# Routing steps of VectorE placed ahead of the weighted sums, and the fetch, columns and weight loads of the overflow blocks reordered, in a fused attention and mixture-of-experts kernel

## The reference

```
x = x + xattn(layernorm(x), ctx)          # x: 4 x 512 x 512, ctx: 4 x 512 x 256
x = x + ffn(layernorm(x))

xattn:  q = ln_head(x @ Wq + bq), 16 heads of 32
        k, v from ctx[:, :-16]  (Wk, Wv); k2, v2 from ctx[:, -16:]  (Wkv_dca)
        out = (softmax(q k^T / sqrt(32)) v + softmax(q k2^T / sqrt(32)) v2) @ Wo + bo
ffn:    E, TOP_K, F, FS = 64, 6, 352, 704;  N = 2048 tokens, C = 2 * N * TOP_K / E = 384
        scores = softmax(x @ gate_w.T); the 6 best of 64, renormalised
        token t goes to slot pos of its expert (counted in token order), dropped if pos >= C
        expert: (silu(rows @ w_gate.T) * (rows @ w_up.T)) @ w_down.T, times the weight,
        added to the token's row
        plus a shared expert of width 704 over all tokens
```

## Time and profile before

| | |
|---|---|
| runs | 1756.02, 1766.42, 1767.89 us; median 1766.42 us |
| the profiled execution | 1762.85 us, of which the span of instructions is 1761.1 us |
| busy in the span | PE 1693.0 us (96%), PEld 1539.8 (87%), DVE 1090.3 (62%), ACT 1028.3 (58%), POOL 757.9 (43%) |
| mean granted clock of TensorE | 0.982 of full speed |
| 830 to 1660 us (experts) | PE busy 830.00 of 830.00 us |
| 1660 to 1761 us (last items and thirds) | PE busy 78.19 of 101.00 us |

### The profile page before, as it was taken

One profiled execution on the slowest core, in us unless ns is written; L12 is line 12 of the kernel. 1 busy time (PEld: TensorE's weight loads), 2 busy tenths in 40 slices (PEclk: granted clock), 3 DMA queues, 4 the chain that ended last, 5 costly groups with the idle time before them and its releaser, 6 DMA issues. The chain is left out here.

```text
span 1761.1 us, 35834 instructions
## 1 busy us (share of the span) xinstructions
PE 1693.0 (96%) x11782; PEld 1539.8 (87%) x11782; DVE 1090.3 (62%) x2157; ACT 1028.3 (58%) x1871; POOL 757.9 (43%) x719
## 2 busy tenths in 40 slices
PE   4899999999999999999999999999999999999995
PEld 3588888888888888989999999999999999999984
DVE  7555656777566665443666666666666666666664
ACT  4567766666545553222566666666666666666664
POOL 7513222334223230242245555555555555455554
PEclk8899999999899999999999999999999999999997
DMA  5543433433222532312577777777777777777766
GB/s 189 160 117 91 119 105 97 121 95 98 83 84 79 177 107 87 122 38 86 181 227 232 209 214 226 218 210 223 223 216 205 228 221 213 222 232 206 215 198 212
DMA packets 149083, 289.87 MB, mean 165 GB/s; under 512 B 29199, under 2 KB 66319, under 8 KB 139649
## 3 DMA queue, kind: packets, MB, share of 16 engines
q1 hardware_dynamic: 116112, 238.21, 41.9%
q0 software_dynamic: 32880, 50.51, 13.7%
HBM read 243.73 MB, written 64.52 MB: 175 GB/s over the span
## 5 line engine op out<-in xcount | busy, mean ns | idle before, releaser
L2188 POOL DMA_INDIRECT out<-y,ids_s x128 | 209.9, 1640 | 280.3 <-ACT y L2323 254.8
L2448 PE MATMUL ps<-xt_hi,gu_hi 128*128 128x256 f32 (+1 forms) x1856 | 303.5, 285 | 0.6 <-issue 0.6
L2448 PE MATMUL ps<-xt_lo,gu_hi 128*128 128x256 f32 (+1 forms) x1856 | 289.8, 278 | 0.0
L2448 PE MATMUL ps<-xt_hi,gu_lo 128*128 128x256 f32 (+1 forms) x1856 | 289.2, 278 | 0.0
L2223 DVE TENSOR_TENSOR gu_lo<-raw_gu,gu_hi 128x1408 fp32r<-128x1408 f32 (+2 forms) x132 | 214.6, 1625 | 112.5 <-ACT gu_hi L2220 109.3
L1121 ACT ACTIVATE prob<-ps 128x512 f32<-128x512 f32 x256 | 152.2, 597 | 191.4 <-PE ps L1428 169.6
L2448 PEld LDWEIGHTS ps<-xt_hi,gu_hi 128*128 128x128 f32 (+1 forms) x1856 | 250.6, 181 | 9.0 <-issue 3.0
L2448 PEld LDWEIGHTS ps<-xt_lo,gu_hi 128*128 128x128 f32 (+1 forms) x1856 | 244.4, 181 | 0.0
L2448 PEld LDWEIGHTS ps<-xt_hi,gu_lo 128*128 128x128 f32 (+1 forms) x1856 | 244.2, 181 | 0.0
L2168 POOL DMA_INDIRECT xg<-h_rows,ids_g x128 | 191.6, 1497 | 115.2 <-POOL ids_g L2163 50.6
L2280 ACT ACTIVATE h_hi<-h 128x256 fp32r<-128x256 f32 (+1 forms) x240 | 100.6, 419 | 224.0 <-DVE h L2349 223.4
(11 more groups left out here) (316 smaller groups left out, 3000.3 us busy)
## 6 DMA issues: line engine op xcount, KB each, us to landing
raw_gu<-in_w_gu SPq DMA_DIRECT2D x71, 1408.0 KB, 6.7
raw_d<-in_w_d SPq DMA_DIRECT2D x71, 512.0 KB
raw_d<-in_w_d SPq DMA_DIRECT2D x71, 192.0 KB
qs<-qk_rows SPq DMA_DIRECT2D x192, 64.0 KB, 2.2
ks<-qk_rows SPq DMA_DIRECT2D x192, 64.0 KB, 2.0
xa<-in_x SPq DMA_DIRECT2D x16, 256.0 KB, 3.0
qk_rows<-k_hi SPq DMA_DIRECT2D x16, 256.0 KB, 2.2
qk_rows<-k_lo SPq DMA_DIRECT2D x16, 256.0 KB, 2.5
```

What stands on the lines that cost most here:

```text
L2188: pool.indirect_dma_start(out=out, out_offset=bass.IndirectOffsetOnAxis(B.ids_s[:, p, k:k + 1], 0), in_=B.y[:, p, k, :], in_offset=None, b ...
L2448: last = pe.matmul(gu_banks(it, c)[half], gu_columns(w, it, half, d, c), x[:, x_p, d, 0:W], start=i == 0, stop=i == len(steps) - 1)
```

## The change

Heads, DVE: in the second quarter of a unit `route_mask` moves ahead of `weighted(n)`; in the third `route_code` ahead of `weighted(n + 1)`; in the fourth `maxima(n + 4, 1)` ahead of `route_slots`. Heads, PE: in unit 10, the only one with a turn of K and no Q product, the turn of K of tile 15 is made after `third_key` instead of before it. After unit 15 the last head's four `weigh` steps come before the first output product and its two waits. Experts: in `scatter` the copy of the row numbers is made before the wait for the scatter before. Thirds: POOL gathers one block further ahead (`gather(3)` right behind item 63's scatters, `gather(b + 4)` in the body), and copies a block's columns behind the scatter of the block before; ACT makes the high part of T0's down weights before item 63's results instead of after them; SP loads the gate and up part of `b + 3` first and then the down part of `b + 2`, each with its own read of the expert number.

```diff
@@ heads, DVE
                 maxima(n + 2, 1)
                 route_top(u - 6)
+                route_mask(u - 6)
                 weighted(n)
-                route_mask(u - 6)
 
                 maxima(n + 3, 0)
                 scales(u)
                 maxima(n + 3, 1)
                 take_pos(u - 6)
+                route_code(u - 6)
                 weighted(n + 1)
-                route_code(u - 6)
 
                 maxima(n + 4, 0)
                 rest(u + 5, k_full, k_hi, k_lo, k_high, k_low, k_out)
+                maxima(n + 4, 1)
                 route_slots(u - 6)
-                maxima(n + 4, 1)
                 route_weights(u - 6)
                 weighted(n + 2)
@@ heads, PE
                 half1(n + 2)
                 route_pos(u - 6)
-                k_turned(u + 5)
+                if tile(u + 6):
+                    k_turned(u + 5)
                 third_key(n + 2)
+                if not tile(u + 6):
+                    k_turned(u + 5)
                 fourth_key(n + 2)
...
             item = net.item
+            weigh(HEADS - 1, 0)
+            weigh(HEADS - 1, 1)
+            weigh(HEADS - 1, 2)
+            weigh(HEADS - 1, 3)
             pe.wait_ge(at_lo.sem, at_lo.value(WAIT1, 1))
             pe.wait_ge(h2T_in.sem, h2T_in.value(WAIT1 - 1, 1))
             wo_half(WAIT1, 0)
-            weigh(HEADS - 1, 0)
-            weigh(HEADS - 1, 1)
             wo_half(WAIT1, 1)
-            weigh(HEADS - 1, 2)
-            weigh(HEADS - 1, 3)
@@ items, POOL: scatter, after
         p = it.half
+        pool.tensor_copy(B.ids_s[:, p, 0:nb], slots_of(it, B.ids)).then_inc(s_copied.sem, 1)
         ...
             pool.wait_ge(added.sem, added.value(it.expert - 1, 16 * nb))
-        pool.tensor_copy(B.ids_s[:, p, 0:nb], slots_of(it, B.ids)).then_inc(s_copied.sem, 1)
...
             thirds["gather_first"](pool, 2)
+            thirds["columns"](pool, FIRST)
             scatter(pool, it)
+            thirds["gather_first"](pool, 3)
             thirds["y_freed"](pool)
@@ items, ACT: after
             thirds["act_x"](act, FIRST + 1)
+            thirds["act_d"](act, FIRST)
             results(it)
-            thirds["act_d"](act, FIRST)
@@ thirds, SP
-        def load(e, b, gu_done, d_done):
-            ...
+        def load_gu(b, done, turn):
+            e = expert(sp, b)
+            sp.wait_ge(done.sem, done.value(turn, 2))
+            sp.dma_start(B.raw_gu[...], ins["w_gu"][...]).then_inc(gu_in[b.p].sem, 16)
+
+        def load_d(b, done, turn):
+            e = expert(sp, b)
+            sp.wait_ge(done.sem, done.value(turn, 1))
+            sp.dma_start(B.raw_d[...], ...)       # two of them
         for k in range(2):
-            load(expert(sp, FIRST + k), FIRST + k, ...)
-        load(expert(sp, FIRST + 2), FIRST + 2, (gu_lo.sem, gu_lo.value(0, 2)), (d_lo.sem, d_lo.value(0, 1)))
+            load_gu(FIRST + k, S.gu_lo, LAST_ITEM.weights - 1 + k)
+            load_d(FIRST + k, S.d_lo, LAST_ITEM.weights - 1 + k)
+        load_gu(FIRST + 2, gu_lo, 0)
 
         def body(b):
-            e = expert(sp, b + 3)
-            load(e, b + 3, (gu_lo.sem, gu_lo.value(b.j + 1, 2)), (d_lo.sem, d_lo.value(b.j + 1, 1)))
+            load_gu(b + 3, gu_lo, b.j + 1)
+            load_d(b + 2, d_lo, b.j)
@@ thirds, POOL
+    def columns(pool, b):
+        e = expert(pool, b)
+        pool.tensor_copy(B.wsl3[:, b.p:b.p + 1], B.w[...]).then_inc(w_copied.sem, 1)
+        pool.tensor_copy(B.ids3s[:, b.p:b.p + 1], B.ids[...]).then_inc(s_copied.sem, 1)
...
-            pool.wait_ge(xt_ready.sem, xt_ready.value(0, 1))
+            pool.wait_ge(xt_ready.sem, xt_ready.value(k - 2, 1))
...
         def body(b):
-            e = expert(pool, b)
-            pool.tensor_copy(B.wsl3[...]) ; pool.tensor_copy(B.ids3s[...])
-            pool.wait_ge(xt_ready.sem, xt_ready.value(b.j + 1, 1))
-            gather(pool, b + 3)
+            pool.wait_ge(xt_ready.sem, xt_ready.value(b.j + 2, 1))
+            gather(pool, b + 4)
             ...        # wait for the scatter of b - 1, y_free, wait for y: as before
                 compute_op=ALU.add).then_inc(added.sem, 16)
+            columns(pool, b + 1)
```

More of the change, by code:

```diff
@@ L2608, in sync @@
     def sync(sp):
-        def load(e, b, gu_done, d_done):
-            src = ins["w_d"][bass.ds(e, 1)].rearrange("a f n -> (a f) n")
-            sp.wait_ge(*gu_done)
+        def load_gu(b, done, turn):
+            e = expert(sp, b)
+            sp.wait_ge(done.sem, done.value(turn, 2))
             sp.dma_start(B.raw_gu[:, b.p].rearrange("p a n -> p (a n)"),
                          ins["w_gu"][bass.ds(e, 1)].rearrange("a p n -> p (a n)")).then_inc(gu_in[b.p].sem, 16)
-            sp.wait_ge(*d_done)
+        def load_d(b, done, turn):
+            e = expert(sp, b)
+            src = ins["w_d"][bass.ds(e, 1)].rearrange("a f n -> (a f) n")
+            sp.wait_ge(done.sem, done.value(turn, 1))
             sp.dma_start(B.raw_d[:, b.p, 0:2, :], src[0:2 * P, :].rearrange("(c p) n -> p c n", p=P)).then_inc(d_in[b.p].sem, 16)
@@ L2619, in sync @@
         for k in range(2):
-            load(expert(sp, FIRST + k), FIRST + k, (S.gu_lo.sem, S.gu_lo.value(LAST_ITEM.weights - 1 + k, 2)),
-                 (S.d_lo.sem, S.d_lo.value(LAST_ITEM.weights - 1 + k, 1)))
-        load(expert(sp, FIRST + 2), FIRST + 2, (gu_lo.sem, gu_lo.value(0, 2)), (d_lo.sem, d_lo.value(0, 1)))
+            load_gu(FIRST + k, S.gu_lo, LAST_ITEM.weights - 1 + k)
+            load_d(FIRST + k, S.d_lo, LAST_ITEM.weights - 1 + k)
+        load_gu(FIRST + 2, gu_lo, 0)
         def body(b):
-            e = expert(sp, b + 3)
-            load(e, b + 3, (gu_lo.sem, gu_lo.value(b.j + 1, 2)), (d_lo.sem, d_lo.value(b.j + 1, 1)))
+            load_gu(b + 3, gu_lo, b.j + 1)
+            load_d(b + 2, d_lo, b.j)
         each(sp, body)
@@ L2637, in gather @@
             bounds_check=N - 1, oob_is_err=False).then_inc(rows_in[b.p].sem, 16)
+    def columns(pool, b):
+        e = expert(pool, b)
+        pool.tensor_copy(B.wsl3[:, b.p:b.p + 1], B.w[:, bass.ds(e * CB + 2, 1)]).then_inc(w_copied.sem, 1)
+        pool.tensor_copy(B.ids3s[:, b.p:b.p + 1], B.ids[:, bass.ds(e * CB + 2, 1)]).then_inc(s_copied.sem, 1)
     def gather_first(pool, k):
@@ L2653, in body @@
         def body(b):
-            e = expert(pool, b)
-            pool.tensor_copy(B.wsl3[:, b.p:b.p + 1], B.w[:, bass.ds(e * CB + 2, 1)]).then_inc(w_copied.sem, 1)
-            pool.tensor_copy(B.ids3s[:, b.p:b.p + 1], B.ids[:, bass.ds(e * CB + 2, 1)]).then_inc(s_copied.sem, 1)
-            pool.wait_ge(xt_ready.sem, xt_ready.value(b.j + 1, 1))
-            gather(pool, b + 3)
+            pool.wait_ge(xt_ready.sem, xt_ready.value(b.j + 2, 1))
+            gather(pool, b + 4)
             if b.q:
@@ L2673, in body @@
                 compute_op=ALU.add).then_inc(added.sem, 16)
+            columns(pool, b + 1)
         many = each(pool, body)
         for p in range(2):
-            pool.wait_ge(rows_in[p].sem, (many + (4 - p)) // 2 * 16)
+            pool.wait_ge(rows_in[p].sem, (many + (5 - p)) // 2 * 16)
         pool.wait_ge(S.added.sem, S.added.value(LAST_ITEM.expert, 16 * nb))
@@ L2720, in scalar @@
         for p in range(2):
-            loads = (many + (4 - p)) // 2
-            act.wait_ge(gu_in[p].sem, loads * 16)
-            act.wait_ge(d_in[p].sem, loads * 32)
+            act.wait_ge(gu_in[p].sem, (many + (4 - p)) // 2 * 16)
+            act.wait_ge(d_in[p].sem, (many + (3 - p)) // 2 * 32)
         act.sem_inc(act_passed, 1)
@@ L2804, in tensor @@
         each(pe, body, many)
-    return dict(how_many=how_many, sync=sync, gather_first=gather_first, y_freed=y_freed, gpsimd=gpsimd, act_gu=act_gu, act_d=act_d,
+    return dict(how_many=how_many, sync=sync, gather_first=gather_first, columns=columns, y_freed=y_freed, gpsimd=gpsimd, act_gu=act_gu, act_d=act_d,
                 act_x=act_x, silu=silu, high=high, scalar=scalar, dve_gu=dve_gu, dve_x=dve_x, dve_d=dve_d, mix=mix,
```

## The result

The changed kernel takes **1803.74 us** (median of 4 runs, 1797.64 to 1807.54), the kernel before 1765.72 in the same comparison: ratio **1.023**, 95% interval 1.0199 to 1.0261. It is slower by 38 us where 8 us less were forecast. The profiled execution's span is 1803.2 us instead of 1761.1, and the mean granted clock 0.957 instead of 0.982.

What follows compares the result with a forecast made beforehand. PE was taken to bound heads and expert items, POOL and its indirect DMAs the last 50 us. Terms -2.6 - 6.3 + 6.9 - 1.2 - 2 = -5.2 us from 1762.85 gave 1758 us, range 1747 to 1773.

Steps and rivals of the forecast that it cites:

- The routing ahead of the weighted sums: Heads, units 11 to 15: route_mask and route_code ahead of the sums make PE wait, +6.9 us (0 to +15).
- argument for a clock that stays up: Heads, against a fall in unit 10: the units after it have the same order and the clock is up.
- Rival 3: Units 11 to 15: new waits lower the clock, 5.5 us a fall; two give 1769 us, five 1785; chance 0.15.
- The turn of K: Unit 10: PE's 0.85 us wait for scaled K goes and the clock stays up, -6.3 us together.
- the strict reading: Unit 10: clock falls only when PE has been idle, so the wait isn't the cause; 1763.5 us, chance 0.22.
- The maxima ahead of the slots: Heads, units 6 to 9: PE's four waits for DVE's last maxima go, -2.6 us.
- Behind unit 15: After the heads: earlier weigh steps fill PE's h2T wait; second output product starts sooner, -1.2 us (0 to -2.5).
- Thirds: POOL's chain at the end: earlier scatters and T3 gather, T1's scatter starts sooner, -2 us (0 to -4).
- The other terms: Maxima -2.6, turn of K -6.3, behind unit 15 -1.2 and thirds -2 us: all the forecast gains.

Runs made afterwards that it cites:

- the filled kernel: Changed kernel plus seven and four unread score products on PE before the second and third quarter's weighted sums, units 10 to 15: 1765.43 us, ratio 0.9984.
- the single fall: Kernel before with route_mask ahead of weighted(n) in unit 12 only: 1773.95 us, ratio 1.0055.
- the thirds alone: Kernel before with only the edits behind the heads (scatter's copy; the thirds' fetches, columns and weight loads): 1759.72 us, ratio 0.9962.
- the kernel with both moves: Kernel before with only route_mask ahead of weighted(n) and route_code ahead of weighted(n + 1): 1808.57 us, ratio 1.0229.
- the code alone: Kernel before with only route_code ahead of weighted(n + 1): 1781.75 us, ratio 1.0111.
- the mask alone: Kernel before with only route_mask ahead of weighted(n): 1811.04 us, ratio 1.0279.
- the kernel with the small filling: Changed kernel plus 3 and 2 unread score products before the second and third quarter's weighted sums, from unit 10 on: 1773.13 us, ratio 1.0028.
- the old turn of K: Kernel before with only the maxima ahead of the slots and the edits behind the heads: 1764.24 us, ratio 1.0001.

## Why the prediction was wrong

**The routing ahead of the weighted sums (+6.9 us) is the step that failed**, and it failed by what it left out. As waits it was right: the filled kernel against the one without both moves shows 1.7, 1.3, 1.3, 1.3 and 1.6 us for units 11 to 15, 7.2 us together. Missing were unit 10 (+1.5 us, which I had passed over) and 1.3 us in units 6 to 9. PE's wait for pv came to 8.3 us where some 8 were forecast, but that is luck: I had two new waits a unit, and in units 12 to 15 there is one, longer than the mask. But the term was taken as the whole price, with nothing in it for the clock, which made some 42 us more (changed against filled, from unit 10 to the items) and was left to a rival with a chance of 0.15. Its rows were on the table: the earlier trace rows show a fall behind a wait of 0.85 us, and I had just worked out two new waits of 1 us or more for each of five units, in the same thin stretch (in the event PE met one a unit: by the third quarter its own work was slow, and DVE was ahead of it). The prediction's argument for a clock that stays up was that it is up in the units after 10, in the same order. But PE's waits for the sums there are 0.49, 0.22, 0.23 and 0.22 us; the new ones, 1.86 and 1.58 to 1.59, are over three times as long.

**Rival 3 happened, and its price was mis-sized too.** Five falls were to give 1785 us; five came, and it was 1804. I took 5.5 us a fall from unit 10, where it begins in the third quarter and lasts 13.7 us. A fall that begins at the second quarter's sums lasts until the next unit's output product, 23.9 us, and costs 10.2 us (unit 13, changed against filled). Price and length are in line, at about 0.4 us lost per us of low clock: 0.43 there, 0.40 for the single fall (8.2 of 20.5 us), 0.38 in unit 10 of the kernel before (6.1 less the wait of 0.85, of 13.7 us). From unit 15 on the changed kernel has 37.1 us of low clock, 3.0 of them of the fall before, against 6.8 in the filled one, and loses 11.8: 0.39. The new fall in unit 10 is cheaper, 2.3 us for 10.2 us, and why stays open. I should have asked where the fall starts and what ends it, instead of carrying over one sum.

**The turn of K (-6.3 us) was right as a sum, in the unit.** 38.5 to 32.4 us in unit 10 is -6.1, of which the wait is 0.85; at its old place the clock falls again. The Trainium skill (TensorE: Matmul & The Clock Gate, "What's actually happening") ties the low clock to an idle TensorE; by the strict reading that I weighed, a wait of 0.85 us with work on both sides would not be the cause. These runs speak against that reading, since without the wait the clock stays in unit 10; but the 1.05 us without a fall shows that such a wait makes a fall possible, not certain. I had the right sum and too plain a cause. In the changed kernel the gain is partly lost again, since the new waits at the sums in unit 10 (0.65 us at 445.16) bring a fall of their own, 10.2 us long: 36.2. And the times of whole runs show less: the maxima and the turn of K, forecast at -8.9 us together, gave -0.22%, which is -3.9 us (-7.8 to 0). In that kernel's profile units 6 to 10 are 7.8 us shorter, but the stretch from unit 15 on is 5.3 us longer, with 13.7 us of low clock in it where the kernel before has none.

**The maxima ahead of the slots (-2.6 us)** gave -1.7: 143.8 instead of 145.5 us in units 6 to 9. The four waits are gone, but PE stands for issue ahead of each of the four output products instead, 1.3 us together where it was 0.3.

**Behind unit 15 (-1.2 us)** nothing is seen. Where the low clock there is 6.8 us long, the stretch takes 56.3 us with the edit and 56.1 without (the kernel with the edits behind the heads alone). The wait for h2T is gone, but there is a new one of 0.7 us at the last head's sums, and that for aT is 2.0 us instead of 1.0: moved, not removed.

**Thirds (-2 us)** gave -3.3 from the items' start to the end in the changed kernel, -2.9 without both routing moves, and -1.3 in the profile of the thirds alone. One profile says little here: six kernels with the old thirds take 1123.4 to 1125.4 us, seven with the new ones 1121.8 to 1124.0, and the means differ by 1.9 us. That is the forecast. The runs of the thirds alone show -0.4%, which is 6.7 us (3.0 to 10.4), more than this sum explains; the rest stays open. The steps are there: T3's gather 3.5 us earlier (1.9 forecast), T1's scatter 2.3 (2.1). The scatter that took 4.75 us takes 1.59 now, and the second is held instead: 2.84 us, ending 1.4 us after DVE's pair. Which of them is held stays open: the first started 0.15 us ahead of DVE's pair when it was held, and starts 0.08 us ahead of it now that it is not. Nor is DVE held by it, which the prediction took as possible: the pair takes 3.24 us, and 3.15 before.

**Faster, same, slower.** The other terms were forecast at -12.1 us together, and the runs don't show that: 1761 us without both moves is 0.1% or 1.9 us below the kernel before (0.3% with 2 unread products in the second and third quarters), with intervals that take in no change. None of these versions is shown to beat the kernel before but the edits behind the heads alone, by 0.4%.

## What to carry to other kernels

Where PE's work is thin, price a new wait on it by what the granted clock does behind it, not by its length: here 1.3 us of DVE work moved ahead of a bank's release in a single unit cost 9.5 us in that unit and the next. If the rows of before show one fall, find its trigger, its start and what ends it, and set each new wait against that. And PE's busy share can't show this; look at the clock column, or at the length of one unchanged instruction.

## What the runs showed of the hardware

- The granted clock falls around a short wait with PE at work on both sides: between the wait's last 0.1 us and 2.7 us after it. All 13 waits of 1.6 to 1.9 us for the weighted sums in units 12 to 15 have a fall at them. Of the shorter ones some do (0.65 and 0.85 in unit 10; 0.70 in unit 11 of the kernel with both moves; 0.74, 1.01, 1.10, 1.20 elsewhere) and some don't (0.69 in unit 11 of the changed kernel; 0.74, 0.76, 0.80, and 1.03 and 1.05 in unit 10). And the wait of 2.0 us for aT behind unit 15 has no fall behind it in any of the four profiles with the clock up at it. So the length doesn't decide, and what does stays open.
- The same code can fall or not. The kernel with the edits behind the heads alone has the heads of the kernel before, and both wait 0.86 us for POOL's join at 620.6 us; in the one the clock then falls for 6.8 us, in the other it doesn't, and their stretches from unit 15 on take 56.1 and 53.9 us. Where it happens, such a fall makes runs of one kernel differ.
- Once low, PE reads 22.00 of 22.00 us busy with the same small matmuls and stays low. The falls in units 12 to 15 last 10.2 us (the code alone) to 41.0 us (the mask alone), most of them 20 to 27. In the timeline above the clock comes back inside the next output product (4.46 us for its 12 matmuls, 2.98 in the kernel with the small filling at full clock).
- Unread matmuls in the hole keep it up: 1.81 us of them in place of 1.86 us of standing is worth 8 to 10 us a unit. What share of the stretch must be filled for that to hold each time wasn't found.
- A POOL scatter of the thirds that starts while DVE runs a subtraction with both inputs in SBUF ends 1.4 to 1.5 us after that subtraction: 2.84 us in the changed kernel, 2.21 without both moves, 2.73 with the old turn of K, instead of 1.6. Twice a pair of subtractions in a row held it, to the same 1.4 to 1.5 us after the second (4.75 us in the kernel before). Two scatters that started within 0.04 us of a subtraction's start were not held.
